# Units of one tile computed by columns like the others, and a clear of 128 scratch columns ahead of gathers 64 to 127

## What is computed

```
e = stack([tbl_f[ids[:, f]] for f in range(32)], axis=1)      # 1024 x 32 x 64, gathered rows
for every pair i < j (496 pairs):  z[b, p] = sum_e (e[b, i, :] @ W[p])[e] * e[b, j, e]
h = concat([z, dense_ctx], axis=1)                            # 496 + 16 = 512
h = relu(h @ W_top1 + b_top1); h = relu(h @ W_top2 + b_top2); y = h @ W_top3
```

## Time and profile before

| what | us |
|---|---|
| median of 3 runs | 444.05 (443.03 to 444.2) |
| the profiled execution, its time | 444.54 |
| its span, first to last instruction | 442.6 |
| busy PE / DVE / ACT / POOL | 383.9 / 367.3 / 351.7 / 325.2 |
| granted TensorE clock, mean | 0.973 |

### The profile page before, as it was taken

How to read it: one execution, slowest core, us unless ns; L and a number is a source line. 1 busy time by engine, 2 the same in 40 slices (tenths; PEclk the granted TensorE clock), 3 DMA queues, 4 the chain that set the end, 5 groups by cost and what they waited for, 6 DMA issues and landing times. The chain is left out here.

```text
span 442.6 us, 9364 instructions
## 1 busy us (share of the span) xinstructions
PE 383.9 (87%) x2384; PEld 208.7 (47%) x2384; DVE 367.3 (83%) x403; ACT 351.7 (79%) x2719; POOL 325.2 (73%) x448
## 2 busy tenths in 40 slices
PE   0368767799999999999899979989999999698978
PEld 0223333545554545555555534555455535334557
DVE  0029979899999899999789996988989898889980
ACT  1199979949999987869697986995879677879972
POOL 5776777777777777778787787887878778885620
PEclk9999889999999999999999998999999999989997
DMA  6999991111122211111111111111111111000000
GB/s 125 170 165 161 161 165 27 27 28 27 29 48 68 49 27 23 22 21 23 20 22 21 20 22 24 20 21 21 22 22 21 21 21 20 19 2 0 3 0 2
DMA packets 44703, 18.91 MB, mean 43 GB/s; under 512 B 39781, under 2 KB 40298, under 8 KB 44650
## 3 DMA queue, kind: packets, MB, share of 16 engines
q1 hardware_dynamic: 36138, 8.86, 15.8%
q0 software_dynamic: 8512, 9.45, 11.1%
HBM read 18.29 MB, written 0.00 MB: 41 GB/s over the span
## 5 line engine op out<-in xcount | busy, mean ns | idle before, releaser
L870 ACT ACTIVATE row_products<-row_products 128x64 f32<-128x64 f32 x1312 | 313.6, 245 | 9.0 <-DVE row_products L799 7.4
L730 POOL DMA_INDIRECT rows<-in_tbl_dram,ids_sb x256 | 243.1, 950 | 85.7 <-POOL pause L724 33.6
L870 ACT ACTIVATION_READ_ACCUMULATOR row_products<-row_products 128x1 f32 x1312 | 251.6, 192 | 0.0
L799 DVE TENSOR_TENSOR row_products<-left,rows 128x1024 f32<-128x1024 f32 x120 | 144.4, 1217 | 19.6 <-PE left L979 19.1
L979 PE MATMUL left<-w_sb,X 64*128 64x512 f32 x480 | 130.4, 634 | 9.7 <-DVE row_products L799 4.2
L789 DVE TENSOR_TENSOR column_products<-left,X 128x1024 f32<-128x1024 f32 x78 | 93.7, 1216 | 12.2 <-PE left L974 12.2
L974 PE MATMUL left<-X,w_sb 64*128 64x256 f32 x720 | 97.2, 395 | 1.7 <-ACT X L854 1.2
L974 PEld LDWEIGHTS left<-X,w_sb 64*128 64x128 f32 x720 | 67.7, 190 | 41.8 <-issue 17.8
L979 PEld LDWEIGHTS left<-w_sb,X 64*128 64x128 f32 x480 | 43.1, 193 | 49.9 <-issue 18.6
L806 DVE TENSOR_TENSOR row_products<-left,rows 128x512 f32<-128x512 f32 (+2 forms) x56 | 37.8, 721 | 26.4 <-PE left L984 25.5
L854 ACT ACTIVATE X<-turned 128x512 f32<-128x512 f32 (+2 forms) x43 | 20.6, 478 | 42.9 <-PE turned L937 42.9
(11 more groups left out here) (38 smaller groups left out, 148.4 us busy)
## 6 DMA issues: line engine op xcount, KB each, us to landing
rows<-in_tbl_dram,ids_sb POOLq DMA_INDIRECT x256, 2.5
w_sb<-in_W_top_dram SPq DMA_DIRECT2D x1, 512.0 KB
w_sb<-in_L_rec_W_dram SPq DMA_DIRECT2D x1, 496.0 KB, 12.3
w_sb<-in_L_rec_W_dram SPq DMA_DIRECT2D x1, 480.0 KB, 11.9
w_sb<-in_L_rec_W_dram SPq DMA_DIRECT2D x1, 464.0 KB
w_sb<-in_L_rec_W_dram SPq DMA_DIRECT2D x1, 448.0 KB
w_sb<-in_L_rec_W_dram SPq DMA_DIRECT2D x1, 432.0 KB
w_sb<-in_L_rec_W_dram SPq DMA_DIRECT2D x1, 416.0 KB
```

Of the source, the lines that this page charges most:

```text
L730: pool.indirect_dma_start(out=rows[:, u % 2 * QT + t, f * D:(f + 1) * D], out_offset=None, in_=tables[f], in_offset=bass.IndirectOffsetOnA ...
L799: ins = nc.vector.tensor_tensor(to, of, fields[:, :, 2 * D * c:2 * D * (c + 4)].to_broadcast([P, 2, BANK]), ALU.mult)
L870: ins = nc.scalar.activation(product, product, ACT.Copy, accum_out=to)
```

## The change

Units 0 and 4 get the pieces of the wide units, 30 column and 2 own pieces each, with 128 sample columns instead of 256 (the banks are filled to half), 64 sums each, and a z_sum of their own; "rest" and "neighbours" go. There are 280 pieces instead of 248, 120 of them by rows instead of 152. A clear of 128 columns now stands ahead of gathers 64 to 127, that of 320 columns from 128 on as before. The planner's numbers move too (`MLP_APART` 8 to 4, `X_WAIT` 16 to 6, and durations), and with them the order.

```
-PAUSES = [(128, 320, 1.6)]
+PAUSES = [(64, 128, 1.45), (128, 320, 1.6)]
...
-    for u, (_, n) in enumerate(UNITS):
-        if n == QT:
-            columns += [("own", u, slot) if isinstance(slot, int) else ("columns", u, slot) for slot in SLOTS]
-        pieces = [("rows", u, t, m, c) for m, c in ROW_UNITS for t in range(n)]
-        if n < QT:
-            pieces += [("rest", u, 0, slots) for slots in REST] + [("neighbours", u, 0)]
-        rows += sorted(pieces, key=lambda x: -least_field(x))
+    for u in range(len(UNITS)):
+        columns += [("own", u, slot) if isinstance(slot, int) else ("columns", u, slot) for slot in SLOTS]
+        rows += [("rows", u, t, m, c) for m, c in ROW_UNITS for t in range(tiles(u))]
...
-MLP_APART = 8
-X_WAIT, MLP_WAIT = 16, 12
+MLP_APART = 4
+X_WAIT, MLP_WAIT = 6, 12
...
-                            ins = nc.tensor.matmul(left[:, s, odd, QB * g:QB * (g + 1)], weights(odd, m, k, 2),
-                                                   X[D * odd:D * odd + D, q % 2 * FP + m, :], start=True, stop=True)
+                            ins = nc.tensor.matmul(left[:, s, odd, width * g:width * (g + 1)], weights(odd, m, k, 2),
+                                                   X[D * odd:D * odd + D, q % 2 * FP + m, 0:width], start=True, stop=True)
...
-                nc.tensor.matmul(z_sum[32 * r:32 * r + 32, :], ones_window[:, 30 - 2 * t:62 - 2 * t],
-                                 column_products[:, v // 2 % COLUMN_PRODS, v % 2, :],
+                r, t, width = v % 4, v % SUMS // 4, columns_of(v // SUMS)
+                nc.tensor.matmul(z_sum[32 * r:32 * r + 32, 0:2 * width], ones_window[:, 30 - 2 * t:62 - 2 * t],
+                                 column_products[:, v // 2 % COLUMN_PRODS, v % 2, 0:2 * width],
```

More of the change, by code:

```diff
@@ L24 @@
 LAST = len(UNITS) - 1
-WIDE = [u for u, (_, n) in enumerate(UNITS) if n == QT]
 NPAIR = F * (F - 1) // 2
@@ L194, in first_gather @@
     return 2 * FP * UNITS[u][0] + 2 * tiles(u) * (FP - 1 - m)
-WITHIN = [sum(x[1] == 0 and least_field(x) >= FP - n for x in make_work()[1]) for n in range(FP + 1)]
+WITHIN = [sum(x[1] == 0 and least_field(x) >= FP - n for pieces in make_work() for x in pieces) for n in range(FP + 1)]
 def pieces_before(g):
@@ L339, in sum_rows @@
                 self.by_act(self.waiting.pop(0))
-            elif gathered is not None and self.rows[self.waiting[0]][0] == "rows" and max(self.pool, gathered - POOL_AFTER, ready) <= now + ACT_SLACK:
+            elif gathered is not None and max(self.pool, gathered - POOL_AFTER, ready) <= now + ACT_SLACK:
                 self.by_pool(self.waiting.pop(0))
@@ L364, in sum_candidate @@
         i = self.sums // SUMS
-        return max(self.pe, self.z_end[WIDE[i - 1]] + SIGNAL) if self.sums % SUMS == 0 and i else self.pe
+        if i and self.sums % SUMS == SUMS - TURN and (self.mlp, self.stage) < (i - 1, 5):
+            return None
+        return max(self.pe, self.z_end[i - 1] + SIGNAL) if self.sums % SUMS == 0 and i else self.pe
     def mlp_candidate(self):
@@ L426, in take_sum @@
     def take_sum(self, begin):
-        self.on_pe("sum", begin, TURN * SUM)
+        self.on_pe("sum", begin, TURN * SUM * tiles(self.sums // SUMS) / QT)
         for v in range(self.sums, self.sums + TURN):
@@ L450, in take_work @@
     def take_work(self, x, begin):
-        length = {"own": OWN, "neighbours": 2 * OWN}.get(x[0], WORK)
+        share = 1 if by_rows(x) else tiles(x[1]) / QT
+        length = (OWN if x[0] == "own" else WORK) * share
         self.on_pe(x[0] == "own", begin, length)
@@ L457, in take_work @@
             begin = max(begin, self.row_end[n - ROW_PRODS])
-        self.dve = begin + (2 if x[0] == "own" else 1) * MULTIPLY
+        self.dve = begin + (2 if x[0] == "own" else 1) * (MULTIPLY if share == 1 else NARROW)
         self.work.append(x)
@@ L521, in make_plan @@
     for n in (0, 1):
-        first = next(w for w, x in enumerate(order.work) if x[0] == "neighbours" or x[0] == "own" and x[2] == 8 - 8 * n)
-        plan.insert(plan.index(("work", first - 4 + 2 * n)), ("wT", n))
+        first = next(w for w, x in enumerate(order.work) if x[0] == "own" and x[2] == 8 - 8 * n)
+        plan.insert(plan.index(("work", first - 3)), ("wT", n))
     return plan, order.work, order.batches
@@ L953, in transpose_z @@
                 for c in (0, 1):
-                    for t in (0, 1):
-                        column, tile, half = (QB * c + P * t, t, c) if tiles(q) == QT else (QB * c + P * t, c, t)
-                        ins = nc.tensor.transpose(turned[:, column:column + P], z_nat[:, q % 2 * QT + tile, P * half:P * half + P], ident[:, :])
+                    for t in range(tiles(q)):
+                        column = columns_of(q) * c + P * t
+                        ins = nc.tensor.transpose(turned[:, column:column + P], z_nat[:, q % 2 * QT + t, P * c:P * c + P], ident[:, :])
                 ins.then_inc(transposed, 1)
@@ L967, in project @@
                 if q == 0:
-                    for m in {"columns": lambda: [m for m, k in x[2]], "rows": lambda: [x[3]], "own": lambda: range(x[2], x[2] + 8),
-                              "rest": lambda: [m for _, m, k, n in runs(x)], "neighbours": lambda: range(FP)}[x[0]]():
+                    for m in [m for m, k in x[2]] if x[0] == "columns" else [x[3]] if x[0] == "rows" else range(x[2], x[2] + 8):
                         pe.wait_ge(w_loaded[m], 32 if m < FP - 1 else 16)
+                width = columns_of(q)
                 if x[0] == "columns":
```

148 lines of the change are left out of this document (38 added, 110 removed).

## The result

The changed kernel took 453.67 us, the median of four runs (452.76 to 454.44). The kernel before took 443.54 us in the same comparison. The ratio is 1.0238, with a 95% interval from 1.0192 to 1.0283. The forecast was 454. A second comparison, later, gave 454.87 us against 441.80, a ratio of 1.0282 (1.0251 to 1.0314).

A forecast was written before the change was run, and what follows sets the result against it. The prediction took late gathers to bound the kernel up to batch (3, 2), then PE's list: gathers +13, shorter list -3.4, tail +0.7. Span 452.9 plus 1.45 gave 454.4, forecast as 454 us, range 446 to 460.

The forecast's parts named there:

- The gathers: POOL's gather stream: clears ahead of gathers 64 to 127 add 14 us, so the later stream comes 13 us later.
- the 25th gather's wait: POOL's wait for the fourth piece, 1.33 us instead of 0.30, should go, since unit 0 begins with cheap column pieces: -1.0.
- batch (3, 2): Last unit's X batch of field pairs 3 and 2: its last gather ends at 390.7, PE transposes it at 392.2.
- stops at the transposes of batch (3, 2): PE, executing its list in order, waits there for the batch's last gather, until 392.2 us.
- PE idle ahead of the batches of units 2 to 4: Sign that the forecast is right: PE waits for gathered data before these units' batches; no size given.
- PE's list behind the batch: PE's work after the last unit's pairs 3 and 2: 38.6 us plus 4.9 for changes of kind, 43.5 in all.
- 2 of packing: Behind that last batch, 2 us added for slots and waits between PE and DVE (0 to 5).
- The tail: From z's transposes to the end: 12.65 us before, +0.7 for eight sums and ACT's copy of z_sum, so 13.35.
- The first one: Rival: clears cost nothing, through hidden slack or a gate on multiplied pieces; 440.3 us, faster by 0.9%; chance 0.06.
- batch (3, 2) is turned at 378: Step of the rival with free clears: PE transposes the last unit's pairs 3 and 2 then; z's transposes come at 425.5.
- the gathers give +13, the shorter list gives -3.4: The forecast's one-line sum: later gathers +13 us, PE's shorter work behind the last unit's pairs 3 and 2 -3.4.

The follow-up runs named there:

- the third group: Follow-up runs: changed kernel with lighter sums or layer 1, and kernel before with shorter clears, on a chip where the kernel before took 500.4 us.

## Why the prediction was right, and where its picture was not

**The gathers.** Predicted 1.43 to 1.50 us each, 14 us of clears and -1.0 from the 25th gather's wait, so 13 us in all. Gather 128 starts 12.3 us later than before, batch (3, 2)'s gather 11.9. The pitch is 1.44, the lower of the two values in the text.

**Batch (3, 2).** Predicted at 392.2, turned at 391.35. The mechanism of this step was wrong in its place: at that batch no row shows that PE "stops at the transposes of batch (3, 2)". PE stopped at pairs 9 and 8 of unit 3, 100 us earlier, and from there its own list ran at the pace at which the gathers came, with one more wait of 0.44 us for data at 371.11. So the sign "PE idle ahead of the batches of units 2 to 4" came true for five batches, 6.6 us in all, and failed at the one on which the sum rests. From the one batch to the other the gathers took 100.1 us and PE 100.5. Counting from either gives the same end, and this is why the number held. The text had not compared the two, so this part of the hit is luck.

**PE's list behind the batch.** Predicted 43.5 us and 2 of packing, from 392.2 to 437.7. It ran from 391.35 to 436.2, 44.9 us. The lengths that it was made of hold: sixteen narrow records take 1.06 us and are two pieces, of which the second starts 0.446 us after the first, where 0.445 was taken; sixteen records of narrow sums take 1.07 for eight sums, 1.00 from start to start with the change of kind in it, where 0.107 a sum and 0.17 for the change give 1.03. The earlier trace rows were near enough. The Trainium skill, TensorE: Matmul & The Clock Gate, section LDWEIGHTS, gives a formula by which eight such loads one behind the other would take 0.85 us a piece. The trace does not agree for loads of the two row halves: it has 0.446. The lighter layer 1 and sums showed by 5.6 to 5.9 of their 6 us that PE bounds this stretch, on the chip of the third group. Layer 3, transposes and the rest were not measured one by one.

**The tail.** Predicted 13.35 us from z's transposes to the end, measured 12.0. Layer 1 took 5.18 us instead of 6.61: the text left it at 6.61 and put 2 to 3 us on it at the full clock. The stretch of layer 1 shows the clock between the two levels, 0.72 on the mean, where the earlier trace rows has 0.50:

```profile
441.20:446.40 5.20, 5.19 (x34) 5.20 (x35) 0.00 (x0) 1.10 (x3) 0.00 (x0) 0.72 0.01 3
```

**DVE.** Predicted near 337 us busy, measured 340.3. Its groups, beside the earlier trace rows:

```profile
L754 DVE TENSOR_REDUCE z_nat<-row_products 128x16 f32<-128x1024 f32 x34 | 40.3, 1209 | 0.1
L738 DVE TENSOR_TENSOR column_products<-left,X 128x512 f32<-128x512 f32 x60 | 39.1, 683 | 30.5 <-PE left L895 30.4
```

The 34 reductions and the 60 narrow multiplies are there at the lengths taken, and ahead of the narrow multiplies DVE waited 30.4 us for PE: what DVE saved turned into waiting, as the text had it.

**The rivals.** The first one (clears cost nothing, 440.3 us) fell, and more than its chance says. With the clears really taken away the time is 448.6, still 1.6% slower than before. The step that failed in it is "batch (3, 2) is turned at 378". It supposed that PE would be there in time. I had added up DVE's list for the whole kernel but PE's only behind the last batch. PE's whole list grew by 14 us of work and 11 of waits for `X`; the run without the clears has PE there at 385.39, and the list added up would have warned of it. For the same reason the last sentence of the sum, "the gathers give +13, the shorter list gives -3.4", describes the path but not the causes. The clears alone, put into the kernel before, cost 13.8 us. The other edits alone cost 6.8. Both together cost 13.1. The overlap, 7.5 us, is at least the whole of the smaller one: the second cost was invisible behind the first.

## What to carry to other kernels

When a delay of the data and a longer list of work come in one change, price each alone, for the whole program: the larger one sets the time, and taking it away leaves the smaller one standing. A batch that is turned right after its data came is not proof of a wait; look for idle time in its row, and if there is none, go up the engine's list until there is some. What one engine saves counts for nothing where another, which takes over part of the work, becomes the bound.

## What the runs showed of the hardware

The kernel before took 442 to 444 us in two comparisons and 498 to 500 in two others, on other chips. In the variants that were profiled there the difference lies mostly in the first 140 us, in gaps of up to 25 us on DVE and ACT that the trace of the core does not explain. What a change costs can differ between such chips: adding 128-column clears to the kernel before cost 13.8 us on the one and nothing on the other, where POOL's gathers waited for multiplied pieces anyway.

A pause on POOL is not always a loss. On one of the slower chips, shorter clears from the 129th gather on made the kernel before 25 us slower, where I had expected a gain. What the pauses protect there was not found.

One wait of 4 us on PE cost 6 us: the granted clock fell to 0.50 behind it, and eight records behind it took 2.08 us instead of 1.13.
